# Carrying a running segment sum from one PSUM bank into the other instead of through an SBUF buffer and an identity product

## What is computed

```python
w_m = (efeat @ W_msg + b_msg).reshape(E, 16, 16)     # per edge a 16x16 matrix
w_a = (efeat @ W_attn + b_attn).reshape(E, 16, 16)
h_src = feat[src][:, :, None]
e1, e2 = w_m * h_src, w_a * h_src
seg_max = segment_max(e2, dst)
ex = exp(e2 - seg_max[dst])
attn = ex / segment_sum(ex, dst)[dst]
ft = segment_sum(e1 * attn, dst).sum(axis=1)
```

## Time and profile before

| | |
|---|---|
| median of three executions | 6938.05 us |
| the profiled execution: own time | 6947.81 us |
| the profiled execution: span from first to last instruction | 6945.9 us |
| mean granted clock of TensorE | 0.839 |
| busy over the span: GpSimd, Vector, TensorE, Scalar | 78%, 74%, 71%, 38% |
| the changed block | about 2942 to 6800 us |

### The profile page before, as it was taken

One profiled execution on the slowest core, in us unless ns is written; L12 is line 12 of the kernel. 1 busy time (PEld: TensorE's weight loads), 2 busy tenths in 40 slices (PEclk: granted clock), 3 DMA queues, 4 the chain that ended last, 5 costly groups with the idle time before them and its releaser, 6 DMA issues. The chain is left out here.

```text
span 6945.9 us, 69675 instructions
## 1 busy us (share of the span) xinstructions
PE 4912.5 (71%) x18115; PEld 2376.1 (34%) x18115; DVE 5160.6 (74%) x7383; ACT 2631.9 (38%) x4866; POOL 5435.1 (78%) x4618
## 2 busy tenths in 40 slices
PE   1277777777777777667777777777777777777771
PEld 1133333333333333333333333333333333333330
DVE  4466666666666666678888888888888888888886
ACT  1122222222222222144554554455554455455453
POOL 6688888888888888388888888888888888888882
PEclk6689888888888888878888888888888888888885
DMA  3222222222222222100000000000000000000002
GB/s 114 56 70 70 68 69 70 67 70 68 53 54 54 54 54 54 25 14 14 14 14 14 14 14 14 14 13 14 14 14 14 14 14 14 14 14 14 14 13 98
DMA packets 386588, 255.80 MB, mean 37 GB/s; under 512 B 243117, under 2 KB 334678, under 8 KB 386305
## 3 DMA queue, kind: packets, MB, share of 16 engines
q0 software_dynamic: 226240, 167.32, 11.5%
q1 hardware_dynamic: 160318, 88.15, 4.3%
HBM read 186.95 MB, written 141.36 MB: 47 GB/s over the span
## 5 line engine op out<-in xcount | busy, mean ns | idle before, releaser
L947 POOL DMA_INDIRECT xg<-x1tab,edge x1920 | 2381.9, 1241 | 550.3 <-issue 535.1
L587 POOL DMA_INDIRECT bg<-btab,mt x1600 | 2112.2, 1320 | 489.9 <-issue 466.1
L697 PE MATMUL pagg<-ohh,stt 125*128 125x512 bf16 x4800 | 1846.2, 420 | 746.1 <-DVE ohh L627 746.1
L1029 PE MATMUL ps<-work,ident 128*128 128x512 f32 x3840 | 2029.1, 654 | 0.1
L1078 DVE TENSOR_TENSOR work<-pw,xg 128x1024 f32<-128x1024 f32 x960 | 1130.8, 1220 | 687.0 <-PE pw L1018 422.8
L698 PE MATMUL pagg<-ohh,stt 125*128 125x270 bf16 x4800 | 1453.7, 303 | 0.0
L1029 PEld LDWEIGHTS ps<-work,ident 128*128 128x128 f32 x3840 | 832.4, 217 | 767.8 <-issue 681.9
L697 PEld LDWEIGHTS pagg<-ohh,stt 125*128 125x128 bf16 x4800 | 510.2, 106 | 1499.3 <-DVE ohh L627 824.5
L678 ACT COPY ohx<-ohl 125x1024 bf16<-125x1024 bf16 x200 | 209.2, 1046 | 1974.0 <-DVE ohl L617 1895.7
L1041 PE MATMUL pt<-identb,parts 128*99 128x128 bf16 x1920 | 231.1, 290 | 909.9 <-POOL parts L938 902.1
L610 DVE TENSOR_TENSOR bg<-bg,e 125x1024 f32<-125x1024 f32 x200 | 245.1, 1226 | 838.9 <-DMA bg<-btab,mt 838.9
(11 more groups left out here) (231 smaller groups left out, 4252.7 us busy)
## 6 DMA issues: line engine op xcount, KB each, us to landing
xg<-x1tab,edge POOLq DMA_INDIRECT x1920
bg<-btab,mt POOLq DMA_INDIRECT x1600
rtab<-zrow SPq DMA_DIRECT2D x56, 384.0 KB
tab<-rtab SPq DMA_DIRECT2D x7, 2048.0 KB, 8.3
etab<-joined SPq DMA_DIRECT2D x200, 66.4 KB
e<-in_edge_attr_dram SPq DMA_DIRECT2D x200, 62.5 KB
e<-in_edge_attr_dram SPq DMA_DIRECT2D x200, 31.2 KB
mt<-meta SPq DMA_DIRECT2D x240, 6.0 KB
```

What stands on the lines that cost most here:

```text
L587: g.indirect_dma_start(bg[:, h, i, :], None, btab, bass.IndirectOffsetOnAxis(ap=mt[:, h, 0, i:i + 1], axis=0)).then_inc(gathered[h], 16)
L697: pe.matmul(pagg[:, 0, :], w, ohh[:, h, i, 0:CUT], start=False, stop=False, skip_group_check=True)
L947: g.indirect_dma_start(xg[:, b % 4, i, :], None, x1tab, bass.IndirectOffsetOnAxis(ap=edge[:, b, i, D:D + 1], axis=0)).then_inc(x_in[b % 4] ...
L1029: pe.matmul(ps[:, b % 2, :], ident[:, :], work[:, b % 4, i, :, :, :].rearrange("p i a o -> p (i a o)"), start=i == 0, stop=False)
```

## The change

The finished sums of tile n-1 stay in their PSUM bank. Vector multiplies them by `corr` of tile n and writes the result straight into the other bank, where the eight identity products of tile n then accumulate on top, without the flag that would start a new sum. The buffer `carry` and the ninth product are gone. Two identity products at the start of the block, on a row of zeros, set up both banks. `carry_on(n)` moves from behind `maxima(n+1)` to between the two halves of `products(n)`, and now waits for `summed` of tile n-1 (and for `st_done` of tile n-2, whose bank it overwrites). Total 0 of tile n waits for `carried` of tile n. Scalar's copy of tile n to `state` now waits for `carried` of tile n+1, so that it and Vector don't use one bank together.

```diff
@@ scalar
-                        act.wait_ge(summed, n + 1)
+                        if isinstance(n, int) and n == NT - 1:
+                            act.wait_ge(summed, n + 1)
+                        else:
+                            act.wait_ge(carried, n + 2)
                         act.copy(state[:, b, C:3 * C], ps[:, b % 2, :]).then_inc(st_done, 1)
@@ tensor
+                for h in range(2):
+                    ins = pe.matmul(ps[:, h, :], ident[:, :], state[:, U - 1, C:3 * C], start=True, stop=True)
+                ins.then_inc(ps_zeroed, 1)
...
                         if i == 0:
-                            wait(pe, st_done, n - 1)
+                            pe.wait_ge(carried, n + 1)
                         if i % H == 0:
                             pe.wait_ge(p_done, 2 * n + i // H + 1)
-                        pe.matmul(ps[:, b % 2, :], ident[:, :], work[:, b % 4, i, :, :, :].rearrange("p i a o -> p (i a o)"),
-                                  start=i == 0, stop=False)
+                        return pe.matmul(ps[:, b % 2, :], ident[:, :], work[:, b % 4, i, :, :, :].rearrange("p i a o -> p (i a o)"),
+                                         start=False, stop=i == J - 1, skip_group_check=True)
...
-                        total(done, J - 1)
-                        n, b, r = done
-                        pe.wait_ge(carried, n + 1)
-                        pe.matmul(ps[:, b % 2, :], ident[:, :], carry[:, b % 2, :], start=False, stop=True).then_inc(summed, 1)
+                        total(done, J - 1).then_inc(summed, 1)
@@ vector
                     v.wait_ge(corr_done, n + 1)
-                    wait(v, st_done, n)
-                    v.tensor_tensor(channels(carry[:, b % 2, :], 2), channels(state[:, (b - 1) % U, C:3 * C], 2),
+                    wait(v, summed, n)
+                    wait(v, st_done, n - 1)
+                    v.tensor_tensor(channels(ps[:, b % 2, :], 2), channels(ps[:, (b - 1) % 2, :], 2),
                                     channels(corr[:, b % 4, :]).unsqueeze(2).to_broadcast([GP, D, 2, D]),
                                     ALU.mult).then_inc(carried, 1)
...
                         maxima(now)
-                    if last := tile(t, q, -1):
-                        carry_on(last)
...
                     if now:
-                        for half in range(2):
-                            products(now, half)
-
-                rounds(v, body, 1, 1)
+                        products(now, 0)
+                        carry_on(now)
+                        products(now, 1)
+
+                rounds(v, body, 1, 0)
```

More of the change, by code:

```diff
@@ L842, in gnn @@
             corr = tsb("corr", [GP, 4, C])
-            carry = tsb("carry", [GP, 2, 2 * C])
             pt = st.enter_context(nc.psum_tensor("pt1", [128, 2, J, 128], BF16))
@@ L871, in gnn @@
             carried = sem("l1_carried")
+            ps_zeroed = sem("l1_ps_zeroed")
             st_done = sem("l1_st_done")
@@ L1068, in _ @@
                 v.sem_inc(w_used, 2)
+                v.wait_ge(ps_zeroed, 1)
                 v.wait_ge(primed, 2)
```

## The result

The changed kernel takes 7030.39 us in the median of four runs (7021.96 to 7033.58), against 6939.0 before (four runs): a ratio of 1.013, 95% interval 1.0112 to 1.0147. It is slower by 91 us where 117 us of gain were forecast.

What follows compares the result with a forecast made beforehand. GpSimd's body was taken as the period, 15.94 us a tile; one block less, 240 tiles x 0.49 = 117 us, took 6947.8 to 6831, and the median 9.8 us lower gave 6821 us; range 6720 to 6990.

Steps and rivals of the forecast that it cites:

- the block: Vector's multiplication into carry, with two SBUF inputs, blocks one GpSimd indirect DMA a tile for 0.487 us.
- the price of the multiplication: Vector's multiplication writing into PSUM: taken as 0.69 us, upper bound 1.22 us.
- the ninth product is worth nothing by itself: On TensorE, dropping it frees at most 1.02 us a tile, while TensorE idles 3.4 to 4.6 us.
- Signs that came all the same: Signs of being right: line 954 mostly 0.94, GpSimd preceded by "issue" alone, multiplication's wait 1.5 to 3 us a tile.
- the sentence on Vector's loop: Vector's loop, 13.06 us without waits, becomes 15.07 and 15.63 us with the stall, just below GpSimd's 15.45.
- The wait for total 7: Before the multiplication, Vector stalls until total 7 of the previous tile ends: 2.01 and 2.57 us in two tiles.
- GpSimd's own 15.45 us: GpSimd's body a tile after the change: 15.94 us less one block of 0.49.
- the 5.1 us to spare: Scalar's copy to state would start no later than now, 5.1 us ahead of the scatter needing it.
- The slower one: Rival: total 7 falls into TensorE's low clock, stall 4.2 us, half of tiles at 17.3 us, 7028 us; chance 0.23.
- The faster rival: Rival: GpSimd gets freer still, Vector's loop sets the pace at 15.07 to 15.63 us, 6720 to 6800; chance 0.24.
- the two rules that the prediction set side by side: Skill's SBUF page: two-SBUF-input tensor_tensor contends with GpSimd instructions reading SBUF; tensor_tensor was not seen to stall GpSimd-issued DMA.
- the four rows of the prediction: Four long GpSimd DMAs, each ending 0.82 us after the Vector instruction met at start plus 0.13; cost 2.6 us together.

Runs made afterwards that it cites:

- experiment 1: The kernel before with only the multiplication's first input moved to the PSUM bank, still filling the carry buffer, ninth product kept: 6833.55 us, ratio 0.9846.
- experiment 9: The changed kernel with GpSimd's subtractions cut to one edge of eight, plus a GpSimd memset of about 1 us ahead of the second: 6858.4 us, ratio 0.9871.
- experiments 4: The changed kernel with GpSimd's two subtractions cut to one edge of eight, leaving out low parts of the other seven: 6798.0 us, ratio 0.9796.
- experiment 7: The changed kernel with GpSimd's two subtractions ahead of the scatter in its body instead of behind it: 7189.25 us, ratio 1.0342.
- experiment 10: The changed kernel with total 7 ahead of products 2 and 3, and the multiplication behind the next tile's first maximum: 6922.48 us, ratio 0.9973.
- experiments 3: The changed kernel with total 7 ahead of products 2 and 3 of the tile after next: 6988.88 us, ratio 1.007.
- experiments 8: The changed kernel with the multiplication back behind the next tile's maxima, PSUM as source and target: 7619.59 us, ratio 1.0968.

## Why the prediction was wrong

**Right: the bound before, and the block.** GpSimd's body was the period, and the multiplication's SBUF source cost it 0.49 us a tile; experiment 1 gives 107 of the 117 us with nothing else changed.

**Right: the price of the multiplication** (0.700 us for 0.69). That the ninth product is worth nothing by itself fits TensorE's idle time, 4.2 us a tile after the change, but no run takes it out alone.

**Signs that came all the same.** The edge gather at 0.94, GpSimd preceded almost only by "issue", a wait of 1.5 to 3 us: these were to show that the forecast was right, and with 0.947 in the median and 2.76 us they all came. A wait of 1.5 to 3 us fits a loop of Vector on either side of GpSimd's body, so it could not tell the two cases apart.

**The step that failed** is the sentence on Vector's loop, "With the stall 15.07 and 15.63 us, mean 15.35. Just below GpSimd's 15.45." The loop is 16.36. The wait for total 7 and its place were as described; two terms of the sum were mis-sized, the second of them put at nothing, and with them Vector's loop became the longer of the two.

*The wait, 2.84 us instead of 2.3* (2.76 of idle, and 0.08 of overlap that a waiting instruction loses). I took it from two tiles of the kernel before, and so with the clock that those had there. (The two tiles were not low ones: the same working over all 233 tiles gives 1.99 us in the mean and 2.77 at most.) Two tiles of the changed kernel show what that hides: the multiplication of one is shown above (5007.59, 3.05 us of idle before it), here is that of the other, then the windows of both from the third `edges` to the multiplication, with the granted clock in the last column but two:

```profile
5056.60 0.70 DVE L1125 TENSOR_TENSOR ps<-ps,corr 128x512 f32<-128x512 f32 x1 [1.85 <-issue]
```

```profile
5001.05:5007.59 6.54, 6.39 (x12) 2.41 (x12) 3.49 (x4) 3.78 (x10) 5.19 (x5) 0.63 0.07 6
5051.25:5056.60 5.35, 5.19 (x12) 2.01 (x12) 3.50 (x4) 3.78 (x10) 4.32 (x4) 0.78 0.06 6
```

At 0.63 for 6.54 us the clock was at the lower of its two levels (0.5, that is 1.2 GHz) for 2 x 0.37 x 6.54 = 4.8 us, and the wait is 3.05; at 0.78 for 5.35 us it was low for 2.4 us, and the wait is 1.85. A tile of experiment 9 with the clock at 1.00 throughout completes the line:

```profile
5025.85:5029.99 4.14, 4.04 (x12) 1.56 (x12) 3.48 (x4) 4.14 (x11) 3.27 (x3) 1.00 0.10 7
```

```profile
5029.99 0.70 DVE L1128 TENSOR_TENSOR ps<-ps,corr 128x512 f32<-128x512 f32 x1 [0.66 <-issue]
```

The wait is 0.66 us at no low clock, and each us of low clock in that stretch adds about half a us (0.66 + 0.5 x 2.4 = 1.86, seen 1.85; 0.66 + 0.5 x 4.8 = 3.06, seen 3.05). A straight line through all 226 tiles of the changed kernel gives nearly the same, 0.79 and 0.48 us for each us, with a spread of 0.07 us around it.

The two tiles of before lie within 0.25 us of the same rule: the clock rose 2.98 and 4.1 us after the third `edges` (before the second of these tiles at 5033.3), which gives 2.1 and 2.7 us of idle; the stalls that I worked out, 2.01 and 2.57, are 1.93 and 2.49 of idle and 0.08 of overlap.

The mean clock of the block is the same before and after, 0.83 and 0.84; it is low at a worse moment. Between the third `edges` and total 7 it was low for 2.96 us in the mean of all tiles before, and is for 4.13 us up to the multiplication now: at half a us for each that is about 0.6 of the 0.85 us between 1.99 and 2.84, and the rest is not traced. What ends TensorE's longest idle used to be `parts` (4.57 and 3.43 us) and now is mostly Vector's `edges` (560.7 us / 226 = 2.5 us a tile ahead of line 1024), nearer to the sum that Vector waits for.

*The clash, 0.39 us instead of nothing.* It is in no term of the prediction, which looked at what Vector's instructions do to GpSimd's and not at the reverse. In order of time in the first of these tiles:

```profile
5012.69 0.45 POOL L933 TENSOR_TENSOR res<-edge,parts 128x128 f32<-128x128 f32 x1
5013.07 1.45 POOL L938 TENSOR_TENSOR parts<-res,parts 128x128 bf16<-128x128 f32 x1
```

```profile
5012.73 2.87 DVE L1110 TENSOR_TENSOR work<-work,state 128x1024 f32<-128x1024 f32 x2
```

GpSimd's two subtractions now fall beside Vector's maxima and subtractions. In this tile the two on Vector take 2.87 us instead of 2.35, line 938 1.45 instead of 0.45. Over the block Vector's lengthening is 2 x (1.355 - 1.219) + (0.532 - 0.485) + two smaller ones of 0.02 and 0.05 = 0.39 us. Before, the two GpSimd instructions met no instruction of Vector but `edges`, whose one input is PSUM, in any tile of the block. `edges` stood right behind the multiplication then; now a product, the maxima and the subtractions stand there, and GpSimd's scatter, with the two subtractions behind it, still starts 1.5 to 3.5 us after the multiplication's end. It can't come earlier than Scalar's copy, which now waits for the multiplication and held it in 47 of 226 tiles; that this is what keeps it at this place is not shown.

The loop is then 13.06 + 2.84 + 0.39 = 16.3 us, against 16.36. Before, the steady period was 16.0; the 15.94 of the prediction has one tile too many in its count, since the last `carry` of all follows 3.7 us behind the one ahead. (16.36 - 16.0) x 240 = 86 us of the 91.

*GpSimd's own 15.45 us* was missed as well, though it doesn't set the time: its body takes 16.36 less at most 0.25 of waits, 16.1 us or a little more. The freer gathers give 8 x 0.068 + 0.05 = 0.6 us a tile, and the clash (0.58 + 0.07 on the two subtractions) and the longer scatter (0.12) take 0.8 back. Nor has Scalar's copy the 5.1 us to spare that the prediction gave it: it now holds GpSimd's scatter in some tiles.

**The rivals.** The slower one was the case that came, and half of its mechanism: the wait did grow with the moment at which the clock rises, and its 7028 us lies 2 us from the measured 7030. That is luck in good part. It had every second tile at a wait of 4.2 us and no clash; the longest of the 226 waits is 3.5 us and the mean 2.84, below the 2.88 that it named as the point from which it decides, and the clash did the rest. The faster rival's freer gathers came too (1.175 us), but GpSimd was no longer the pace.

**What the clash drags along is shown in size and not in cause.** With no clash the wait is 2.18 and 1.76 us (experiments 4 and 9) and PEclk 0.89 and 0.88; with 0.39 us it is 2.76 and 0.84; with 0.5 us, 3.35 and 0.80 (experiment 7). All four waits follow from the time that the clock was low between the third `edges` and the multiplication: 2.92, 2.34, 4.13 and 5.39 us a tile give, in the same order, 2.1, 1.8, 2.7 and 3.4 us by the working above. Why it was low for longer is open. It isn't the amount of TensorE's idle time, which is 4.1, 4.5, 4.2 and 4.3 us a tile in these four. It isn't the lateness of `parts` either: TensorE waits for `parts` in neither of experiments 4 and 7, and their waits are 1.2 us apart.

The rule of the Trainium skill (SBUF, Who interferes with whom) that a `tensor_tensor` with two SBUF inputs contends with GpSimd instructions that read SBUF, and one with a single SBUF input doesn't, agrees with the traces in both directions here: 1.43 to 0.95 us on GpSimd in experiment 1, 1.22 to 1.36 us on Vector after the change. Of the two rules that the prediction set side by side experiment 1 thus decides for the first: a `tensor_tensor` does hold the indirect DMAs that GpSimd issues.

## What to carry to other kernels

When a change removes the wait or the block that held one engine back, or moves an instruction, work out where every other engine's instructions will then stand against each other, and price the clashes both ways; a duration from the trace holds only for its neighbours there. A wait for TensorE that is read off the trace contains the clock of that moment: take several tiles, and note how long the clock was low in each. An instruction that has to wait goes behind the work that is ready: here the same multiplication one product later turned +91 us into -152, and with the sum it waits for issued earlier, into about -200.

## What the runs showed of the hardware that was not expected

- An indirect DMA of GpSimd is held by a Vector `tensor_tensor` with two SBUF inputs until that instruction ends, and needs 0.82 us from there, whatever had passed before: the four rows of the prediction fit within 0.02 us. In the whole block before, 902 of the 925 DMAs whose start plus 0.13 us falls into such an instruction fit within 0.01 us; the other 23 fall into its first 0.16 us and are not held.
- `scalar_tensor_tensor` holds them too. Before the change nearly all of its 225 cases at line 1097 fell into its first 0.04 us and took 0.95 us, which looks like the opposite; in experiment 10 a gather met `gap` 0.28 to 0.37 us after its start in 224 tiles, and ended 0.82 us after it. One of them, 5007.77 + 0.48 + 0.82 = 5009.07 against 5009.06:

```profile
5007.77 0.48 DVE L1108 SCALAR_TENSOR_TENSOR gap<-state,mt 128x256 f32<-128x256 f32 x1
```

```profile
5007.92 1.14 POOL L947 DMA_INDIRECT xg<-x1tab,edge  x1 [0.30 <-issue]
```

- The other way round, GpSimd's `tensor_tensor` with SBUF inputs lengthens Vector's two-input instructions: 1.22 to 1.36 us in the mean here, 1.44 in experiments 3 and 7.
- A Vector multiplication from PSUM and SBUF into PSUM, 128x512 f32, takes 0.700 us in the changed kernel (0.69 in experiments 8 and 10), against 0.685 from SBUF into SBUF.
